# Four graph networks on one core: POOL scales the own rows and adds the constants row in the attention layers' slot passes

## The reference

```
def _gat_layer(x, src, dst, ea, W, We, a_s, a_d, a_e, b, g, beta):
    h = x @ W
    e = ea @ We
    alpha = h @ a_s
    alpha = alpha[src] + (h @ a_d)[dst] + e @ a_e
    alpha = jax.nn.leaky_relu(alpha, NEG_SLOPE)
    alpha = _segment_softmax(alpha, dst, N)
    out = jax.ops.segment_sum(h[src] * alpha[:, None], dst, num_segments=N) + b
    mu = out.mean(-1, keepdims=True)
    var = ((out - mu) ** 2).mean(-1, keepdims=True)
    return (out - mu) * jax.lax.rsqrt(var + LN_EPS) * g + beta
```

## Time and profile before

| | us |
|---|---|
| median of 3 runs | 6403.81 |
| lowest and highest run | 6377.07, 6413.65 |
| profiled execution, span from first to last instruction | 5398.9 |
| median of the runs less the span | 1004.9 |
| four slot passes, which start near 1100, 1612, 2124 and 2640 us of the span | some 175 to 205 each |

### The profile page before, as it was taken

The page is one execution under the profiler, slowest core; times in us unless marked ns, Lnnn a source line. Parts: engine busy times, 40 slices in busy tenths (PEclk is TensorE's granted clock), DMA queues, the critical chain, the costliest instruction groups (busy, mean ns, idle before and its releaser), DMA issues. The chain is left out here.

```text
span 5398.9 us, 104328 instructions
## 1 busy us (share of the span) xinstructions
PE 3821.1 (71%) x23663; PEld 3143.4 (58%) x23663; DVE 3792.3 (70%) x10843; ACT 3176.1 (59%) x11279; POOL 2893.9 (54%) x2759
## 2 busy tenths in 40 slices
PE   6355889566747685768575768678688787977775
PEld 5354778565537453645474545456577676866665
DVE  2575889688849784978596767677567675756666
ACT  2022889577848684868482323356577685655554
POOL 0466766603650463066205867676376564757776
PEclk8698999888979797979676767677799998988777
DMA  8898999556955694578463446555489797872221
GB/s 183 129 301 269 383 362 278 176 148 179 283 175 149 203 283 154 156 229 278 149 184 126 131 129 189 167 158 177 165 282 303 248 305 238 246 189 66 62 66 57
DMA packets 918273, 1074.23 MB, mean 199 GB/s; under 512 B 202780, under 2 KB 565066, under 8 KB 917107
## 3 DMA queue, kind: packets, MB, share of 16 engines
q1 hardware_dynamic: 763570, 890.24, 50.5%
q0 software_dynamic: 90944, 180.06, 13.6%
q10 hardware_dynamic: 63556, 1.81, 1.6%
HBM read 509.54 MB, written 566.14 MB: 199 GB/s over the span
## 5 line engine op out<-in xcount | busy, mean ns | idle before, releaser
L2358 POOL DMA_INDIRECT H<-gat_rows,src_i x784 | 804.1, 1026 | 1032.9 <-POOLq L79 620.9
L1909 POOL DMA_INDIRECT s_G<-sage_rows,src_i x588 | 602.4, 1025 | 369.6 <-issue 161.0
L1695 POOL DMA_INDIRECT r_G<-rel_rows,idx x392 | 441.7, 1127 | 216.8 <-issue 110.2
L1708 PE MATMUL r_t<-r_oh,relv 8*128 8x512 f32 x294 | 227.4, 862 | 217.5 <-issue 77.2
L2547 PE MATMUL p_M<-Wg,p_hT 128*128 128x132 f32 x2352 | 336.6, 287 | 63.1 <-DVE p_res L2604 48.8
L1743 ACT ACTIVATE r_mT<-r_t 128x512 f32<-128x512 f32 x147 | 87.4, 594 | 460.4 <-PE r_t L1711 460.1
L2547 PEld LDWEIGHTS p_M<-Wg,p_hT 128*128 128x128 f32 x2352 | 290.3, 192 | 113.0 <-issue 96.0
L2604 DVE SCALAR_TENSOR_TENSOR p_res<-p_M,p_rr,cg 128x132 f32<-128x132 f32 x1176 | 333.8, 346 | 2.5 <-PE p_M L2547 1.4
L1304 PE MATMUL d_S<-ones,d_sqT 128*128 128x1 f32 x1568 | 224.3, 264 | 144.0 <-DVE d_ve L1449 144.0
L2686 PEld LDWEIGHTS p_pl_p<-Wn,p_pl_h 128*128 128x128 f32 x1568 | 205.9, 198 | 201.8 <-ACT p_pl_h L2780 154.9
L2686 PE MATMUL p_pl_p<-Wn,p_pl_h 128*128 128x128 f32 x1568 | 225.3, 289 | 132.6 <-ACT p_pl_h L2780 132.4
(11 more groups left out here) (482 smaller groups left out, 12286.0 us busy)
## 6 DMA issues: line engine op xcount, KB each, us to landing
gat_rows<-p_res SPq DMA_DIRECT2D x294, 264.0 KB
sage_rows<-p_pl_s SPq DMA_DIRECT2D x294, 256.0 KB
gat_rows<-x_row SPq DMA_DIRECT2D x98, 536.0 KB
gat_rows<-d_res SPq DMA_DIRECT2D x147, 264.0 KB
d_hs<-gat_rows SPq DMA_DIRECT2D x147, 256.0 KB
s_hT<-sage_slots_t SPq DMA_DIRECT2D x147, 256.0 KB
slot_rows<-H SPq DMA_DIRECT2D x49, 544.0 KB, 11.5
x_x<-in_x SPq DMA_DIRECT2D x98, 256.0 KB
```

Source lines behind the costliest of these rows:

```text
L1695: pool.indirect_dma_start(self.G[:, g % 4, k, :], None, table, bass.IndirectOffsetOnAxis(index[:, c:c + 1], 0), bounds_check=bound, oob_is ...
L1708: pe.matmul(pt[:, :], kn.relv[:, l, :], self.oh[:, b.m % self.Y, :], start=True, stop=False)
L1909: pool.indirect_dma_start(self.G[:, g % 4, k, :], None, kn.st[self.l], bass.IndirectOffsetOnAxis(kn.idx[:, c:c + 1], 0), bounds_check=boun ...
L2358: pool.indirect_dma_start(kn.H[:, c, 0:width], None, table, bass.IndirectOffsetOnAxis(index[:, c:c + 1], 0), bounds_check=bound, oob_is_er ...
```

## The change

POOL gets two steps in the slots passes. `own` (lag 0) multiplies a block's own rows, all 512 columns in one instruction, by the weights spread over the features (`fan`); `out` (lag 7, passes l = 0 to 2) adds the constants row. In POOL's turn `out` stands first. ACT's `own` and DVE's `out` go. Semaphores, tiles and lags are the same.

```diff
+            @block.gpsimd
+            def _(pool):
+                def own(b):
+                    landed(pool, hin, b)
+                    pool.tensor_tensor(hs[:, b.s4], hs[:, b.s4], fan(self.pl[:, bass.ds(b.n * KT, KT)], D), ALU.mult).then_inc(ow, 1)
+
+                def out(b):
+                    done(pool, rsc, b)
+                    pool.tensor_tensor(res[:, b.s4], res[:, b.s4], spread(self.cg[:, l + 1, :], KT), ALU.add).then_inc(om, 1)
+
+                times(pool, [(own, 0)] if end else [(out, 7), (own, 0)], KG)
+
...
-                def own(b):
-                    landed(act, hin, b)
-                    for k in range(KT):
-                        last = act.activation(hs[:, b.s4, k, :], hs[:, b.s4, k, :], ACT.Copy, scale=self.pl[:, bass.ds(b.n * KT + k, 1)])
-                    last.then_inc(ow, 1)
...
-                core = [(deviation, 6), (square, 4), (own, 0)]
+                core = [(deviation, 6), (square, 4)]
...
-                def out(b):
-                    done(v, rsc, b)
-                    v.tensor_tensor(res[:, b.s4], res[:, b.s4], spread(self.cg[:, l + 1, :], KT), ALU.add).then_inc(om, 1)
...
-                    times(v, once + [(out, 7), (run_sums, 3), (scale, 6), (weigh, 1), (variance, 5)], KG)
+                    times(v, once + [(run_sums, 3), (scale, 6), (weigh, 1), (variance, 5)], KG)
```

## The result

| kernel | median us, runs | ratio to the kernel before, 95% interval |
|---|---|---|
| before | 6403.81, 9 runs | |
| changed | 6437.95, 9 runs | 1.0057, 1.0040 to 1.0074 |

The change makes the kernel slower by 0.57%, 36.5 us. The forecast was slower, 6475 us; the measured time lies in its range, and 2 us inside the lower end of its own narrower one, 6436 to 6545.

The account below looks back on a forecast made before the run. DVE and ACT were taken to bound the middle passes, DVE alone the last. Strict turns with POOL add 56 us there and 15 us in the last pass: 6404 + 71 = 6475 us, range 6290 to 6545.

Parts of the forecast that it names:

- What bounds the kernel: Slot passes: DVE and ACT level and near full in the middle passes (3.31 us a block), DVE alone in the last (4.23).
- POOL's durations: POOL's multiplication and addition: 1.2 us each, 2.4 us a block, between 0.84 and 1.57 us each.
- The disputed term: POOL's operations and DVE's weighing, all reading two SBUF tensors: strict turns, 3.7 us a middle block, against 2.6 without exclusion.
- The opposite bound: Middle passes: POOL and DVE don't touch each other, so a block takes 2.6 us, set by POOL's 2.4 + 0.18.
- The middle passes' size: Three passes of 49 blocks: each block grows from 3.31 to 3.69 us under strict turns, +56 us.
- the handover of 0.18: Middle blocks under strict turns: one handover of 0.18 us added to POOL's 2.4 and the weighing's 1.11 us.
- The last pass: POOL's multiplication would run against DVE's weighing or norm: 0.3 us a block, +15 us, within bounds of 0 and 59.
- The new chain of waits: From DVE's scale through ACT and POOL to the weighing: 4.8 us fits in two turns of 3.31, so costs nothing.
- The clock rival: Middle passes: strict turns leave PE idle longer and lower its clock, +37 us more, 6512 us; 9% chance.
- Balance, 16%: Slot passes: turns are taken, but POOL's operations last only 1.0 to 1.1 us, some 6415 us; 16% chance.
- Relief, 31%: Middle passes: no exclusion, a turn of 2.6 us, -104 us, last pass 0, 6300 us; 31% chance.
- The signs: Weighing longer where it overlaps POOL, 32 or 33 scans in 1130 to 1250 us, DVE's idle time ended by POOL.

Follow-up runs that it names:

- the PSUM kernel: The changed kernel with the weighing's first input taken from a PSUM tile in place of SBUF from block 8 on; ratio 0.9899 to before, -64 us.
- the middle passes alone: The changed kernel, but ACT keeps the own rows' multiplication in the last pass; ratio 1.0036 to before, +23 us.
- the moment in the last pass: The changed kernel, with POOL's multiplication in the last pass waiting for DVE's norm of eight blocks back; ratio 1.0029 to before.

## Why the prediction was right, point by point

- **What bounds the kernel.** Right. DVE and ACT were level in the middle passes, DVE alone in the last. The addition alone on POOL showed it: with DVE relieved, ACT is full and a block takes 2.90 us.
- **POOL's durations.** I had set 1.2 us each between 0.84 and 1.57. The addition is 1.31, the multiplication 1.04: 2.35 together against 2.4.
- **The disputed term.** Right in its side, and now shown from both engines: the weighing collides with two inputs in SBUF and not with one in PSUM, and POOL's operation must read a tensor, not only write one. The rule of the Trainium skill, "SBUF — State Buffer", section "Who interferes with whom", has a DVE instruction with two SBUF inputs contend with a GpSimd instruction that reads SBUF, and not with one that only writes it; the trace agrees in both parts (1474 ns beside the reading operations, 357 beside the memsets). The opposite bound, 2.6 us a block, was just as real: the PSUM kernel has 2.56.
- **The middle passes' size.** This is the mis-sized term: 3.69 - 3.31 = 0.38 us a block over all 147, +56 us. Measured are +22.5, in two parts. The first four blocks of the three passes lose 11 us together, a start that the sum didn't look at. In the rest a block takes 3.37 to 3.43 us, some 0.1 over before's. POOL's 2.35 and the weighing's 1.10 in a row are 3.45, so the handover of 0.18 should not have been there; in the timeline, the three POOL operations from 1644.91 on start within 0.2 us of each other's ends. Even without it the row of turns is an upper bound: with half of the own rows on POOL it asks for 3.07 and 2.79 is measured. How much of an instruction's length is really exclusive, no run shows.
- **The last pass.** Forecast +15 us by 0.3 us a block; measured 16.5, of which 4 at the start and the rest as 0.28 us a block over the other 45. The multiplication fell into the weighing alone: the norm stays at 692 ns throughout. The wait behind the norm shows that it is the phase. The size within its bounds of 0 and 59 us was a choice, and that it came so near is luck.
- **The new chain of waits.** Costed at nothing, rightly: the PSUM kernel has the whole chain, scale to scaling to addition to multiplication to weighing, and runs at 2.56 us a block. In the changed kernel POOL does stand 36.8 us of 120 for ACT's scaled rows; without the collisions that costs nothing.
- **The clock rival.** Its sign showed, its price did not. The granted clock fell to 0.79 to 0.90, but the scan's waits for PE are 2.4 to 5.9 us in 120. The traces part clock from collisions: in blocks 8 to 44 of the three middle passes, a block takes 3.50 us in the stretches granted 1.2 GHz and 3.37 in those at 2.4, in the two kernels with the same middle passes (the middle passes alone, the moment in the last pass) 3.46 and 3.40, and 3.41 and 3.46. Before it is 3.33 at 2.4 GHz. So the loss stands at the full clock, and what the lower level adds is not clear of the scatter. The rival's price of 4.2 us was also misread: it divides the ACT instructions of a pass's start by the 11 of a full block, where not all steps run yet; the weighing passes the first eight blocks of that pass in 24.2 us, 3.0 each.
- **Balance, 16%.** Turns with shorter operations, some 6415 us. Its premise failed, since the addition takes 1.31 us, but its time is nearer to the measured 6438 than the forecast's 6475. The direction is clear of noise (+26 to +47 us); that the time is still inside the forecast's narrower range, by 2 us, is in part luck.
- **Relief, 31%.** It fell for the change, but its size was about right. It had -104 us; with the weighing's first input in PSUM the traces' passes are 78 us shorter, with the first eight blocks of each still colliding, and with memsets on POOL 97 us.
- **The signs.** The weighing is longer where it meets POOL, as foretold. But the scan's count in 120 us is 36, not 32 or 33, and DVE's idle time is not ended by POOL: a collision doesn't show as waiting, it makes DVE's instruction longer, so DVE looks busy (116.5 us of 120) with less work to do.

## What to carry to other kernels

Work moved to an idle engine is not free if that engine reads SBUF beside instructions of another that can't share the reads with it. Add the two-input SBUF reads of DVE and all of POOL's reading operations as if they were one engine's work, and compare that sum with the engine relieved. Where the shared reads were the bound, the sum was an upper one: 3.45 us for some 3.4 measured, 3.07 for 2.79. A sum that fits is not enough: the multiplication alone asks for 1.04 + 1.10 + 0.71 = 2.85, and a block still took 3.33 to 3.59, because DVE was near full already and each collision lengthened its own round. Move the piece that also takes a two-input read off DVE: the addition alone does (0.71 us off DVE for 1.31 on POOL) and gained 51 us, the multiplication alone relieves only ACT and cost 76, and both together cost 36.5. Where the sum fits, the moment still matters: one wait that puts POOL's read beside a DVE instruction with a PSUM input took the loss of a pass away but for 3 us. And look at a pass's start, where full buffers let the new engine run without a pause: 15 of the change's 39 us are lost there.

## What was not expected

- Half of the change was worse than all of it: the multiplication alone on POOL costs 76 us, and DVE keeps a second two-input instruction (709 ns, up to 1589) to collide with.
- On POOL the columns cost by what is read: 525 ns for 512 columns written, 614 with one input, 1.04 us with one tensor and one number spread over the features. The addition of 528 columns with a whole row as the second input is 1.31 us: 2.5 ns a column against 2.0. The two differ in the operation as well, and no run parts that from the inputs.
- A DVE tensor_scalar with one tensor input in SBUF, 272 ns, also waited, in the kernel in which POOL's only work is the 1.31 us addition: all 8 that met it took 1039 ns or more. So two tensors in SBUF are not what every DVE instruction needs to collide.
- Two profiles of one kernel had spans of 5398.9 and 6359.4 us, with all four slot passes alike within 0.3 us. Compare stages, and check the profiled execution's span against the runs.
